# DLRM tower, one core: the table's three bf16 parts as truncated views, and a new order of the start

## What is computed

```python
e = stack([tbl_f[ids[:, f]] for f in range(16)], axis=1)     # 2048 x 16 x 16, fp32
# x0: 2048 x 39 x 16, alpha: 624 x 16, w: 16 x 16 x 16, hv: 16 x 16
A  = repeat(x0, 16, axis=1)
Bm = repeat(e, 39, axis=2).reshape(2048, 624, 16)
z  = einsum('bnh,bnd,nk,khd,kd->bkh', A, Bm, alpha, w, hv)   # 2048 x 16 x 16
h  = relu(concat([z, dense_ctx]) @ W_top1 + b_top1)          # 512
h  = relu(h @ W_top2 + b_top2)                               # 256
y  = h @ W_top3
```

## Time and profile before

| | us |
|---|---|
| median of 3 runs | 178.87 (178.35 to 182.15) |
| the profiled execution | 179.62 |
| its span, first to last instruction | 177.8 |
| busy PE, DVE, POOL, ACT | 163.5, 142.1, 109.2, 56.0 |

### The profile page before, as it was taken

One profiled execution on the slowest core, in us unless ns is written; L12 is line 12 of the kernel. 1 busy time (PEld: TensorE's weight loads), 2 busy tenths in 40 slices (PEclk: granted clock), 3 DMA queues, 4 the chain that ended last, 5 costly groups with the idle time before them and its releaser, 6 DMA issues.

```text
span 177.8 us, 5038 instructions
## 1 busy us (share of the span) xinstructions
PE 163.5 (92%) x2139; PEld 122.4 (69%) x2139; DVE 142.1 (80%) x166; ACT 56.0 (31%) x175; POOL 109.2 (61%) x116
## 2 busy tenths in 40 slices
PE   6667899947999999799999999999999999999993
PEld 1335788635896788396968696969686967776771
DVE  2926879999999849999999989996999799495000
ACT  3516445212053152312440244123402341441231
POOL 2777777777777771777777777777777776000000
PEclk9999999999999999999999999999999999999999
DMA  5969799979999997888488939594569440000000
GB/s 90 318 118 245 231 251 381 222 174 251 393 372 221 336 307 167 299 298 234 72 347 269 221 122 339 178 235 100 203 204 223 84 184 7 4 0 0 0 4 0
DMA packets 15084, 34.25 MB, mean 193 GB/s; under 512 B 6618, under 2 KB 10582, under 8 KB 11990
## 3 DMA queue, kind: packets, MB, share of 16 engines
q1 hardware_dynamic: 10162, 31.51, 58.4%
q0 software_dynamic: 3584, 0.92, 5.1%
q10 hardware_dynamic: 1316, 1.50, 2.8%
HBM read 33.88 MB, written 0.04 MB: 191 GB/s over the span
## 4 chain that ended last, share of the span: by engine, by line
PE 81%; DVE 6%; DMA 3%; issue 3%; ACT 3%; SPq 2%; DVEq 0%; ACTq 0%
PE bank L873 18%; PE bank L792 16%; PE bank L798 14%; PE bank L840 14%; PE bank L861 5%; PE bank L785 5%; DMA table<-tbl_dram 3%; DVE prod L623 3%; PE bank L896 2%; PE bank L882 2%; SPq L391 2%; PE bank L821 1%; PE bank L815 1%; DVE e L512 1%; PE bank L806 1%
## 5 line engine op out<-in xcount | busy, mean ns | idle before, releaser
L466 POOL DMA_INDIRECT e<-tbl_dram,ids_all x112 | 109.0, 973 | 40.6 <-issue 32.9
L623 DVE TENSOR_TENSOR prod<-x,bank 128x2048 f32<-128x2048 f32 x40 | 90.4, 2277 | 3.0 <-PE bank L861 2.5
L873 PE MATMUL bank<-prod,m_w 128*32 128x256 f32 x640 | 38.6, 382 | 3.1 <-DVE prod L623 3.1
L840 PEld LDWEIGHTS bank<-parts,onehot 125*128 125x128 bf16 x864 | 29.9, 99 | 4.9 <-issue 2.3
L840 PE MATMUL bank<-parts,onehot 125*128 125x64 bf16 (+1 forms) x864 | 31.6, 197 | 0.5 <-DVE onehot L481 0.4
L792 PE MATMUL bank<-tower,w_z 128*128 128x256 f32 x128 | 31.4, 389 | 0.0
L873 PEld LDWEIGHTS bank<-prod,m_w 128*32 128x32 f32 x640 | 19.1, 109 | 17.6 <-issue 4.8
L798 PE MATMUL bank<-tower,w 128*128 128x256 f32 x128 | 30.5, 381 | 0.1
L792 PEld LDWEIGHTS bank<-tower,w_z 128*128 128x128 f32 x128 | 23.1, 190 | 5.2 <-ACT tower L702 2.3
L798 PEld LDWEIGHTS bank<-tower,w 128*128 128x128 f32 x128 | 23.3, 191 | 3.4 <-ACT tower L655 0.5
L655 ACT ACTIVATE tower<-bank,b_w 128x256 f32<-128x256 f32 x32 | 13.4, 470 | 29.3 <-PE bank L792 27.3
(11 more groups left out here) (48 smaller groups left out, 53.6 us busy)
## 6 DMA issues: line engine op xcount, KB each, us to landing
x<-x_dram SPq DMA_DIRECT2D x16, 1024.0 KB, 5.2
x<-x_dram SPq DMA_DIRECT2D x16, 512.0 KB, 5.6
ids_b<-ids_half_dram SPq DMA_DIRECT2D x7, 576.0 KB, 6.7
e<-tbl_dram,ids_all POOLq DMA_INDIRECT x112, 5.4
prod<-windows_c_dram ACTq DMA_DIRECT2D x1, 768.0 KB, 6.8
prod<-windows_c_dram ACTq DMA_DIRECT2D x1, 512.0 KB, 5.4
w_z<-w_z_dram SPq DMA_DIRECT2D x1, 512.0 KB
w<-w_dram SPq DMA_DIRECT2D x1, 512.0 KB
```

The lines of the kernel that those rows point to most:

```text
L466: nc.gpsimd.indirect_dma_start(out=e[:, tile, f * D:(f + 1) * D], out_offset=None, in_=t[f"tbl_{f}"][:, :], in_offset=bass.IndirectOffsetO ...
L623: nc.vector.tensor_tensor(prod[:, s % NPROD, :].rearrange("p (q b) -> p q b", q=HP), x0[:, tile % NX, :].rearrange("p (q b) -> p q b", q=H ...
L840: made = nc.tensor.matmul(o_bank[i % 2][:, at:at + m * D], onehot[:, n % 2, g, HOT.index(f), tile * P:(tile + 1) * P], parts[:, part, KT_A ...
L873: made = nc.tensor.matmul(z_bank[q * ZW:(q + 1) * ZW, a * HB:(a + 1) * HB], m_w[:, UNIT_OF[g], hp * ZW:(hp + 1) * ZW], prod[:, s % NPROD, ...
```

## The change

The three parts become views. The upper 16 bits of an fp32 number are a bf16 number, cut off instead of rounded. So part 0 is `table` itself, read as bf16 with a step of two elements (4 bytes); `rest` = `table` minus part 0 is an fp32 tensor whose upper halves are part 1, and `low` = `rest` minus part 1 is written as bf16. Two DVE subtractions per pack make `rest` and `low` (`split_table`); `fill_rest`, `cut_rest`, `keep_part` and `minus` go. The picks' 108 matmuls per half stay, and two of three now have a moving operand with that step. The order of the start changes on DVE, SP, PE and ACT.

```diff
-PLANE_STEPS = {1: [BEFORE, BEFORE], 2: [4, 4], ...
+PLANE_STEPS = {1: [0, 0], 2: [4, 4], ...
...
+        def upper(of):
+            return of[:].rearrange("p k d -> p (k d)").bitcast(bf16).rearrange("p (k d h) -> p k d h", d=D, h=2)[:, :, :, 1]
+
+        parts = [upper(table), upper(rest), low[:]]
...
             sp.dma_start(ids_rows[1], ids_half[1:IDS:NH, :]).then_inc(ids_stored[0], 16)
+            sp.dma_start(ids_all[:, 2:, :], ids[:, 2:, :]).then_inc(in_ids, 16)
             load_table(1)
-            sp.dma_start(ids_all[:, 2:, :], ids[:, 2:, :]).then_inc(in_ids, 16)
+            load_x0(0)
             sp.wait_ge(ids_stored[0], 16)
             load_ids(1)
-            load_x0(0)
             sp.dma_start(h4_mask[:], ...
+            sp.wait_ge(gathered[0][0], 16 * 2 * len(GATHERED[0][0]))
+            load_x0(1)
             for n in range(2, NH):
                 sp.dma_start(ids_rows[n], ids_half[n:IDS:NH, :]).then_inc(ids_stored[1], 16)
-            sp.wait_ge(gathered[0][0], 16 * 2 * len(GATHERED[0][0]))
-            load_x0(1)
...
+            def split_table(p):
+                ks = pack_slice(p)
+                dve.wait_ge(in_table[p], 16 * len(TABLE_LOADS[p]) * len(PACKS[p]))
+                nc.vector.tensor_tensor(rest[:, ks, :], table[:, ks, :], parts[0][:, ks, :], ALU.subtract).then_inc(rest_made[p], 1)
+                dve.wait_ge(rest_made[p], 1)
+                nc.vector.tensor_tensor(low[:, ks, :], rest[:, ks, :], parts[1][:, ks, :], ALU.subtract).then_inc(low_made[p], 1)
...
-            nc.vector.tensor_scalar(minus[:], ident, -1.0, None, ALU.mult).then_inc(minus_made, 1)
...
-            dve.wait_ge(in_ids, 16)
-            make_mask(1, 2, NT)
-            for plane in PLANES[BEFORE]:
-                make_plane(*plane)
+            split_table(0)
             dve.wait_ge(v_made, 1)
...
+            split_table(1)
             mask_rows(0)
             mask_rows(1)
             sum_rows(0)
             sum_rows(1)
-            mask_rows(2)
-            mask_rows(3)
-            sum_rows(2)
-            sum_rows(3)
+            dve.wait_ge(in_ids, 16)
+            make_mask(1, 2, NT)
...
             for s in range(STEPS):
                 multiply(s)
+                if s == 1:
+                    mask_rows(2)
+                    mask_rows(3)
+                    sum_rows(2)
+                    sum_rows(3)
```

More of the change, by code:

```diff
@@ L146 @@
 BEFORE = -1
-PLANE_STEPS = {1: [BEFORE, BEFORE], 2: [4, 4], 3: [7, 8], **{n: [UH * (n - 1) - 4, UH * (n - 1) - 3] for n in range(4, NH)}}
+PLANE_STEPS = {1: [0, 0], 2: [4, 4], 3: [7, 8], **{n: [UH * (n - 1) - 4, UH * (n - 1) - 3] for n in range(4, NH)}}
 PICK_STEPS = {1: [BEFORE, 2, 3], 2: [5, 5, 6], 3: [9, 10, 11], **{n: [UH * (n - 1) - 2, UH * (n - 1) - 1, UH * (n - 1)] for n in range(4, NH)}}
@@ L247, in program @@
         table = sb("table", [TP, KT_ALL, D], fp32)
-        parts = sb("parts", [TP, 3, KT_ALL, D], bf16)
+        rest = sb("rest", [TP, KT_ALL, D], fp32)
+        low = sb("low", [TP, KT_ALL, D], bf16)
         ids_all = sb("ids_all", [P, NT, S], i32)
@@ L322, in program @@
         alpha_rest = sem("alpha_rest")
-        table_split = [sem(f"table_split_{p}") for p in range(2)]
-        table_left = [sem(f"table_left_{p}") for p in range(2)]
-        minus_made = sem("minus_made")
+        rest_made = [sem(f"rest_made_{p}") for p in range(2)]
+        low_made = [sem(f"low_made_{p}") for p in range(2)]
         zeros_set = sem("zeros_set")
@@ L723, in _ @@
                 empty(job)
-            keep_part(0, 0)
-            keep_part(0, 1)
+            for ft in range(2):
+                keep_ab(ft)
             act.wait_ge(in_w_hv, 16)
@@ L729, in _ @@
             made.then_inc(v_made, 1)
-            keep_part(0, 2)
-            keep_part(1, 0)
-            keep_part(1, 1)
-            for ft in range(2):
-                keep_ab(ft)
-            keep_part(1, 2)
             for ft in range(2, FT):
@@ L808, in fill_t @@
                 made.then_inc(t_filled, 1)
-            def fill_rest(p):
-                pe.wait_ge(in_table[p], 16 * len(TABLE_LOADS[p]) * len(PACKS[p]))
-                rows = table[:].rearrange("p k d -> p (k d)")
-                at = KT_AT[PACKS[p][0]] * D
-                for lo, hi, bank in rest_pieces(p):
-                    nc.tensor.matmul(bank[0:TP, 0:hi - lo], ident[0:TP, 0:TP], rows[:, at + lo:at + hi], start=True, stop=False,
-                                     skip_group_check=True)
-            def cut_rest(p, n):
-                pe.wait_ge(table_split[p], n + 1)
-                for lo, hi, bank in rest_pieces(p):
-                    made = nc.tensor.matmul(bank[0:TP, 0:hi - lo], minus[0:TP, 0:TP], flat_part(p, n)[:, lo:hi], start=False, stop=n == 1,
-                                            skip_group_check=True)
-                made.then_inc(table_left[p], 1)
             def pick_rows(i):
@@ L840, in pick_rows @@
                                     made = nc.tensor.matmul(o_bank[i % 2][:, at:at + m * D], onehot[:, n % 2, g, HOT.index(f), tile * P:(tile + 1) * P],
-                                                            parts[:, part, KT_AT[f] + g * m:KT_AT[f] + (g + 1) * m, :], start=first,
+                                                            parts[part][:, KT_AT[f] + g * m:KT_AT[f] + (g + 1) * m, :], start=first,
                                                             stop=g == G - 1 and part == 2, skip_group_check=True)
@@ L924, in _ @@
                 sum_ab(ft)
-            pe.wait_ge(table_split[1], 3)
+            pe.wait_ge(low_made[1], 1)
             pick_rows(2)
             pick_rows(3)
+            pe.wait_ge(in_ident, 16)
             turn_windows(0, 0)
@@ L931, in _ @@
             sum_m(0)
+            sum_m(1)
+            sum_m(2)
             for i in PICKS[BEFORE]:
                 pick_rows(i)
-            sum_m(1)
-            sum_m(2)
             for s in range(STEPS):
```

34 lines of the change are left out of this document (4 added, 30 removed).

## The result

The changed kernel took 182.68 us, the median of 4 runs (181.51 to 183.84), against 179.63 of 4 runs of the kernel before; the ratio is 1.0155 [1.011, 1.0201]. The forecast of 177.6 us had the wrong sign, and the result lies above its range, which ended at 180.7. The profiled execution took 183.44 us, its span is 181.6, 3.8 more than before.

What follows compares the result with a forecast made beforehand. DVE was taken to bound the start, PE the stretch from 74.4 to 170 us. A 1.3 us sooner start off the profiled 179.62 gave 178.3, against the median 177.6 us; range 175.4 to 180.7.

Steps and rivals of the forecast that it cites:

- DVE's queue sets the start and PE the rest: DVE bounds the start up to 41.3 us, PE 74.4 to 170 us; 1.3 us gained at product 5 reach the end.
- the views cost PE nothing: Picks on PE: 40,960 columns read in steps of 4 bytes take no longer; all picks stay at 31.6 us.
- Rival A: Picks on PE: stepped operand read at half rate, 17.1 us more, run 192.6 us; chance 0.10, in full or in part.
- What waits for others on this way: Start: checks of loads and PE work that DVE's new queue needs; x tile 0 at 17, first windows at 19.7.
- rival C: Start: a load replaces the wait, pack 1 at 15.7 or x tile 0 after 21.8; no gain, 178.9 us; chance 0.16.
- I let the last of the pair land at the same time, 14.22: Second split: pack 1, now issued behind the late ids, lands at 14.22, as the ids did before.
- The bound of 15.7: Second split: pack 1, its issues ending near 9.9, lands at 15.7 at the latest.
- I subtract 0.2: Behind product 2: pick 5 ends near 32.6, DVE is through at 32.4; 0.2 us off, leaving 1.3 us of gain.
- rival B: Start: PE's clock rises later, after standing still from about 10 to 12; 1.8 us slower than before, 180.7; chance 0.06.
- Picks and sums then run almost back to back: Argument against a late clock rise: PE is busy almost without a break from 12 to 18 us.
- Gone at no gain: Start: removing ACT's six casts and PE's fp32 fills and cuts gains nothing, since both engines had idle time.
- D: Second split: pack 1 is there by 12.7, DVE does not wait; gain 2.8 us, 176.1 us; chance 0.12.

Runs made afterwards that it cites:

- wait_later: The changed kernel with ACT's wait for `h4_mask` moved behind `spread_e(0, 0)`, no DMA moved; ratios 1.0111 and, run again, 1.0045 to the kernel before.
- h4_first: The changed kernel with the DMA of `h4_mask` issued ahead of x tile 0; ratio 1.0001 to the kernel before.
- pick5_first: The changed kernel with pick 5 ahead of contractions 0 and 1 on PE; ratio 1.0151 to the kernel before.
- pads: The changed kernel with 19 zero matmuls in PE's gaps (behind pick 3, ahead of pick 4 and behind it); ratio 1.0102 to the kernel before.
- views_only: The kernel before with the views alone, old order everywhere; ratio 1.0029 to the kernel before.
- all repairs: The changed kernel with `h4_mask` ahead of x tile 0, pack 1 ahead of late ids, pick 5 ahead of contractions, and zero matmuls; ratio 0.9974 to the kernel before.

## Why the prediction was wrong

- **Right: that DVE's queue sets the start and PE the rest.** Product 5's shift of 3.5 us arrived at the end as 3.8, and that of 2.4 between the two profiles of `wait_later` as 2.2. It did not hold in every profile: `h4_first` and `pick5_first` lost 2.3 and 1.7 us more behind it. The subtractions took 0.79, 0.81, 0.86 and 0.86 us against 0.78 and 0.85, and from 23.31 to 33.15 no step was off by more than 0.1.
- **Right but for 0.3 us: the views cost PE nothing.** Rival A is false: 33.15 us of picks in all, under the 35 that would have shown it, and 1.2% behind 40 us.
- **Wrong: "What waits for others on this way".** For product 0 I weighed x tile 0 and the first windows ("0.6 us of cover"), and let ACT go with the sums. ACT also waits for `h4_mask`, and that term was not in the sum. The diff leaves the mask where it was, behind x tile 0 and `ids_b`, and makes ACT want it 4.0 us sooner: a landing that was hidden before is one that product 0 waits for. With the wait moved (`wait_later`) or the mask issued first (`h4_first`) product 0 starts at 21.36 and 21.10 instead of 23.31. It is rival C's kind with a load I did not name. Product 0 waited 2.1 us, 1.7 of it for the mask and 0.4 for a turn at 1.2 GHz; C had "the gain is nothing".
- **Wrong: "I let the last of the pair land at the same time, 14.22".** Equal bytes did not land in equal time in the other order: the last of the pair, now pack 1, was there at 15.36. With pack 1 ahead of the ids it was there at 13.03. The bound of 15.7 held it; the value missed 1.1 us, of which 0.9 reached the end of the second mask.
- **Mis-sized: pick 5, "I subtract 0.2".** The mechanism was right and the number too at full clock (0.24 in `pads`, 0.30 in `wait_later`). The "1.9" for the contractions came from a row at clock 1.00; they took 3.37, and the wait was 2.03.
- **Half right: rival B.** I gave the clock 0.06, and only as a late rise after the gap at 10 to 12. The first picks did run at half rate (12.10 to 15.1), inside cover. What cost were new falls, at 22.0 and 32.3, behind idle stretches that the new order gives PE: 2.15 us ahead of the first, 1.19 and 0.72 ahead of the second. "Picks and sums then run almost back to back" says nothing of that stretch, and "Gone at no gain" took PE's fp32 work as worth nothing: in `views_only` its going brought a fall at 21.3 and two late picks.
- D is false: pack 1 was not there by 12.7.

In the profile the 5.1 us between the 178.3 that the sum gives for a profiled execution and the measured 183.44 are 0.9 for pack 1, 2.1 for product 0's windows and 1.8 for pick 5 under the clock, with 0.3 behind product 5, as much as the stepped picks cost there. The places are shown by the repairs' profiles. In the times two steps are: all repairs beside the change (1.0122 to 0.9974), and pack 1 and pick 5 first once the mask's wait is moved (1.0111 to 1.0025). With the mask's wait moved and the zero matmuls the ratio comes from 1.0155 and 1.0122 down to 1.0031. How that divides between mask and clock is not shown, since `wait_later` lies between them with two ratios, 1.0111 and 1.0045.

## What to carry to other kernels

When a new order lets an engine come to an instruction sooner, list every semaphore that it waits for up to there, also for loads whose place in the queue does not change: a landing that was hidden may not be any more. Let a wait stand directly ahead of the instruction that needs it. When work is taken off an idle PE or DVE work is put ahead of PE's, price PE's next steps at 1.2 GHz too. A start made 3 us sooner meets the next bound, here x tiles and gathers.
